# One table of the order for the whole program, and experts and Mamba as two lanes with buffers of their own

## What is computed

```python
x = x + 0.5 * ffn(LN(x)); x = x + mamba(LN(x)); x = x + 0.5 * ffn(LN(x))      # LN without weights

def ffn(x):                       # the same weights in both uses
    h = causal_conv3(layernorm(x)); q, k, v = split(h @ attn_w)               # 16 heads of 8
    x = x + softmax(causal(rope(q) @ rope(k).T / sqrt(8))) @ v @ proj_w
    h = layernorm(x); e = argmax(h @ router_w)                                # one of 4 experts for each token
    return x + (silu(h @ wv[e][:, :512]) * (h @ wv[e][:, 512:])) @ expert_proj[e]

def mamba(x):                     # convolution of 4 taps and silu give xs, B, C; 4 heads of 64, state of 64
    z, xs, B, C, dt = project(x @ W_in)
    for t in range(512): h = dA[t] * h + dt[t] * xs[t] * B[t]; y[t] = h @ C[t] + D * xs[t]
    x = x + rmsnorm(y * silu(z)) @ W_out
    return x + silu(rmsnorm(x) @ w1 + b1) @ w2 + b2
```

## Time and profile before

| | |
|---|---|
| median of 3 runs | 1969.23 us (1958.37 to 1971.66) |
| profiled execution, its own time | 1961.06 us |
| its span | 1959.3 us |
| TensorE matmuls busy | 1472.6 us, 75% |
| TensorE weight loads busy | 779.5 us, 40% |
| VectorE busy | 1202.9 us, 61% |
| ScalarE busy | 808.2 us, 41% |
| GpSimd busy | 386.4 us, 20% |
| mean granted clock of TensorE | 0.848 of full speed |
| attention core C0, first to last exponential | 81.7 to 129.3 us |
| C1 | 230.1 to 305.4 us |
| C2 | 403.8 to 489.0 us |
| C14 | 1710.6 to 1763.8 us |
| C15 | 1835.6 to 1889.5 us |
| Mamba of rows 3, 4, 5, 6: `mu` made at | 780.9, 985.3, 1192.7, 1397.9 us |

### The profile page before, as it was taken

How to read it: one execution, slowest core, us unless ns; L and a number is a source line. 1 busy time by engine, 2 the same in 40 slices (tenths; PEclk the granted TensorE clock), 3 DMA queues, 4 the chain that set the end, 5 groups by cost and what they waited for, 6 DMA issues and landing times. The chain is left out here.

```text
span 1959.3 us, 30365 instructions
## 1 busy us (share of the span) xinstructions
PE 1472.6 (75%) x11328; PEld 779.5 (40%) x11328; DVE 1202.9 (61%) x2807; ACT 808.2 (41%) x1266; POOL 386.4 (20%) x396
## 2 busy tenths in 40 slices
PE   1366686578787898788978897879788987773855
PEld 0133343334343454444534453435344544332423
DVE  5344654476649675876678667867685648543532
ACT  0132243334353445444545454355545451441432
POOL 1001131031113211231223022402141214011111
PEclk9578598868788899899979897899888987886877
DMA  5203000202020303031301130032103100302101
GB/s 166 27 2 62 1 2 17 46 1 33 22 42 2 48 29 62 2 43 27 62 8 27 22 74 16 7 43 49 35 7 43 31 22 6 42 22 39 24 9 33
DMA packets 75807, 61.43 MB, mean 31 GB/s; under 512 B 6800, under 2 KB 71824, under 8 KB 75664
## 3 DMA queue, kind: packets, MB, share of 16 engines
q1 hardware_dynamic: 71568, 51.10, 14.8%
q0 software_dynamic: 4096, 8.40, 1.4%
HBM read 19.23 MB, written 14.55 MB: 17 GB/s over the span
## 5 line engine op out<-in xcount | busy, mean ns | idle before, releaser
L907 ACT ACTIVATE prob_mem<-aring 128x1024 f32<-128x1024 f32 x320 | 325.5, 1023 | 208.9 <-PE aring L639 203.3
L1266 DVE TENSOR_REDUCE mx<-aring 128x2 f32<-128x1024 f32 (+2 forms) x384 | 316.9, 861 | 138.3 <-PE aring L622 136.1
L597 PE MATMUL aring<-ramps,spots 64*128 64x128 bf16 (+1 forms) x2560 | 182.3, 223 | 137.1 <-DVE mx L1266 56.9
L729 PE MATMUL wring<-wv,scratch 128*128 x448 | 238.2, 646 | 6.8 <-ACT scratch L944 3.6
L597 PEld LDWEIGHTS aring<-ramps,spots 64*128 64x128 bf16 x2560 | 87.9, 99 | 339.8 <-issue 201.5
L582 PE MATMUL obank<-prob_mem,vx 128*9 128x512 f32 (+3 forms) x2048 | 199.7, 491 | 25.3 <-ACT prob_mem L907 15.0
L859 ACT ACTIVATE scratch<-wring 128x512 f32<-128x512 f32 x224 | 97.9, 437 | 179.7 <-PE wring L734 127.4
L1080 POOL DMA_INDIRECT got<-od,slot x64 | 63.3, 988 | 491.8 <-DMA od<-scratch 468.3
L1377 DVE SCALAR_TENSOR_TENSOR scratch<-scratch,wring 128x512 f32<-128x512 f32 x112 | 76.9, 686 | 135.0 <-ACT scratch L949 133.9
L639 PE MATMUL aring<-stq,stk 50*128 50x512 bf16 (+3 forms) x1024 | 141.5, 335 | 0.0
L622 PE MATMUL aring<-stk,stq 48*128 48x128 bf16 (+3 forms) x1024 | 137.0, 330 | 0.0
(11 more groups left out here) (211 smaller groups left out, 2429.2 us busy)
## 6 DMA issues: line engine op xcount, KB each, us to landing
hb<-hd SPq DMA_DIRECT2D x16, 448.0 KB, 3.5
stq<-high SPq DMA_DIRECT2D x96, 64.0 KB
stk<-high SPq DMA_DIRECT2D x96, 64.0 KB
stq<-mid SPq DMA_DIRECT2D x64, 64.0 KB
stk<-mid SPq DMA_DIRECT2D x64, 64.0 KB
od<-scratch SPq DMA_DIRECT2D x16, 256.0 KB, 3.0
od<-scratch SPq DMA_DIRECT2D x16, 192.0 KB, 2.1
x<-in_x SPq DMA_DIRECT2D x8, 256.0 KB, 2.8
```

The costliest lines, as they stand in the source:

```text
L597: pe.matmul(dst, spots[rows, 2 * by_key + part, :], ramp, start=(part == 0), stop=False, skip_group_check=True)
L729: last = pe.matmul(ring[:], hTd[:, u * P:(u + 1) * P], wv[:, expert[u], o:o + DFF], start=True, stop=True)
L907: act.activation(prob_mem[:, k], ring[:], ACT.Exp, scale=float(HD) ** -0.5).then_inc(freed, 1)
L1266: last = dve.tensor_reduce(mx[:, j, h0 + q:h0 + q + 3:2], ring[:, :, c:c + w], AX_X, ALU.max)
```

## The change

The lanes are now seven: Mamba (number 3) and the experts (number 4) have one each, and G and L become 5 and 6. `plan` joins the lanes of all turns first, and `ORDER` has one digit for each of the 1952 steps, so no two turns need be alike. Which steps exist, and the order within each lane, are as before.

Because a Mamba step may now stand beside an expert step, `yv`, `yaT` and `ob` get tiles of their own, `hTd` takes the place of `hb` itself, `scratch` shrinks to 4 x 512 columns for `MV` and `ga`, and Mamba's `Xd`, `Xw`, `Gm`, `gb` and `gt` move into tiles of Mamba that are free at that time. With this go: `Xw` in two instructions, the two `Square`s of the Mamba tail both behind `Y1`, the load of `hb` behind the last `value` of the pass before, and a wait of `xsT` for the two `z` steps.

```diff
-            steps("M", i - 1, first=M_CUT) + steps("E", i - LAG - 1, 1) + steps("E", i) + steps("M", i, last=M_CUT),
+            steps("M", i - 1, first=M_CUT) + steps("M", i, last=M_CUT),
+            steps("E", i - LAG - 1, 1) + steps("E", i),
...
 ORDER = (
-    "11311121331233131321133311233133112302113113112331111331021033003310031131131501033331113110331031130311131311"
...
+    "00000000000000111111111111111101011111111111110111111111011101001111112111212121202221016101111111140110141404"
...
-    out = []
-    for i in range(-1, rows + LAG + 1):
-        lanes = [iter(lane) for lane in turn(i, rows)]
-        out += [(lane, *step) for lane in map(int, ORDER) if (step := next(lanes[lane])) is not None]
-        assert all(next(lane, None) is None for lane in lanes)
+    turns = [turn(i, rows) for i in range(-1, rows + LAG + 1)]
+    lanes = [iter([step for steps in turns for step in steps[lane] if step is not None]) for lane in range(len(turns[0]))]
+    out = [(lane, *next(lanes[lane])) for lane in map(int, ORDER)]
+    assert all(next(lane, None) is None for lane in lanes)
...
-        scratch = sb("scratch", [P, 8 * T])
-        hTd = scratch[:, 0:UNITS * P]
-        at = UNITS * P
-        yv = [scratch[:, at + T * k:at + T * (k + 1)] for k in range(2)]
-        yaT = [scratch[:, at + T * (2 + k):at + T * (3 + k)] for k in range(2)]
-        ob = scratch[:, 6 * T:6 * T + UNITS * P].rearrange("p (u c) -> p u c", u=UNITS)
+        hTd = hb[:].rearrange("p u c -> p (u c)")
+        yv = [sb(f"yv{k}", [P, T]) for k in range(2)]
+        yaT = [sb(f"yaT{k}", [P, T]) for k in range(2)]
+        ob = sb("ob", [P, UNITS, P])
...
+        scratch = sb("scratch", [P, 4 * T])
+        MV = scratch[:].rearrange("p (j h t) -> p j h t", j=4, h=MH)
...
-        Xd = scratch[:, 4 * T:6 * T].rearrange("p (j h d) -> p j h d", j=4, h=MH)
-        Xw = scratch[:, 6 * T:8 * T].rearrange("p (j h d) -> p j h d", j=4, h=MH)
+        Xd = [zt[k][:].rearrange("p (j h d) -> p j h d", j=2, h=MH) for k in range(2)]
+        Xw = [cpad[1 + k][:, 3:].rearrange("p (j h d) -> p j h d", j=2, h=MH) for k in range(2)]
...
-        Gm = sb("Gm", [P, 4, P])
+        Gm = uT[:].rearrange("p (j c) -> p j c", j=4)
...
-        gb, gt = ([scratch[:, T * (q + k):T * (q + k + 1)] for k in range(2)] for q in (4, 6))
+        gb, gt = ([conv[:, q + k] for k in range(2)] for q in (0, 2))
...
                 if n > 0:
-                    sp.wait_ge(s["w_filled"], w_fill["E", n - 1]["hb", 1] + 1)
+                    sp.wait_ge(s["w_filled"], w_fill["E", n - 1]["value", UNITS - 1] + 1)
...
-                    elif kind in ("Y0", "Y1"):
-                        c = int(kind == "Y1")
-                        act.wait_ge(s["m_gT"], 2 * i + c + 1)
-                        act.activation(gq[c][:], gT[c][:], ACT.Square).then_inc(s["m_gq"], 1)
+                    elif kind == "Y1":
+                        act.wait_ge(s["w_filled"], filled)
+                        for c in range(2):
+                            act.wait_ge(s["m_gT"], 2 * i + c + 1)
+                            act.activation(gq[c][:], gT[c][:], ACT.Square).then_inc(s["m_gq"], 1)
...
-                        pool.wait_ge(s["e_stored"], 32 * (ffn(0, i, NB) + 1))
...
+                        if c == 0:
+                            w_used(dve, step["z", 0], step["z", 1])
```

36 lines of the change are left out of this document (26 added, 10 removed).

## The result

The changed kernel takes 1730.84 us, median of four runs (1725.48 to 1734.06), against 1963.8 us (1955.4 to 1971.66) for the kernel before on the same chip. The ratio is 0.8812, 95% interval 0.876 to 0.8863. So it is faster by 233 us, where 139 were forecast and 1765 us was the lower end of the range. The direction was right, the size was not.

A forecast was written before the change was run, and what follows sets the result against it. TensorE, busy 1472.6 us, bounds the kernel; an order can win its 486.7 us idle. Fill −66, steady −55 and drain −18 sum to −139: 1961 to 1820 us, range 1785 to 1855 (54%), 1765 to 1895 for 8 in 10.

The forecast's parts named there:

- Buffers: The new buffer sharings and the later wait of the `hb` load, whole kernel: costed at nothing.
- Opening and end: Stretches to 129.3 us and from 1763.8 us on: 0, as C0 runs alone and the tail order stays.
- Two reloads of `hb` that nothing can cover: In the tail from C14 on: their 28.0 us of TensorE waits would stay.
- Fill: 129.3 to 574.1 us: −66 us, waits −58, clock −12, new `mlp` wait +4, with C1 and C2 spread over other lanes.
- mlp: New TensorE wait right behind `up` 3, about 2 us a row: +4 in the fill, +10 steady, +2 in the drain.
- Steady: 574.1 to 1598.5 us, five turns: −55 us, waits −71, `mlp` +10, VectorE beside GpSimd +6; `mx` drains stay.
- the +6 for VectorE beside GpSimd: Steady turns: GpSimd's Mamba products slow VectorE work beside them, some two such hits more a turn, +6 us.
- I take −12 for the 318.9 us of the stretch: Fill: a higher clock takes 12 us off TensorE's 318.9 us of busy time there.
- the sum treats each wait apart: Whole forecast: the −139 us adds up each wait's saving separately.
- Rival 1: More than forecast: denser order lifts the fill's clock to 0.9, −35 instead of −12, steady waits to 60: 1770 us, 15%.
- Rival 2: Steady gain lost to VectorE slowed beside GpSimd: 1865 us, 1875 with the gain gone, 1905 with half the fill; 20%.
- Rivals 3 and 4: 3: no change within 1%, idle time only moves, 6%; 4: slower, gates' banks held longer, 2000 us, 5%.

The follow-up runs named there:

- e1_old_order: Changed kernel with its new buffers and waits but the old list, five loads of `hb` 11 entries later: 1972.02 us, ratio 1.0001 to the kernel before.
- r2: Changed kernel with 54 of its 64 shifts moved right behind the last maximum of their group: 1883.97 us, ratio 0.9593 to the kernel before.
- r3: Changed kernel with 25 shifts moved up to about their old distance behind the last maximum: 1799.13 us, ratio 0.9138 to the kernel before.
- e2: Changed kernel with the new list up to the end of C4, then the old order: 1898.41 us, ratio 0.9629 to the kernel before.
- e3: Changed kernel with the old list up to the end of C4, then the new order: 1857.36 us, ratio 0.9425 to the kernel before.
- e4_one_lane: Changed kernel with Mamba and experts in the one sequence of the kernel before, other lanes near their new places: 2122.41 us, ratio 1.0808.
- c3_before_warm_long: Kernel before with idle transposes ahead of TensorE's long pauses only, none ahead of the shifts: 1982.5 us, ratio 1.0062.
- c1_before_warm: Kernel before with 836 idle transposes, four ahead of each of 64 shifts and more ahead of long pauses: 1954.71 us, ratio 0.993.
- c4_again: Changed kernel with four idle transposes ahead of each shift, run a second time: 1729.51 us, ratio 0.8768 to the kernel before.
- after_again: Changed kernel as it is, run again in the same session on another chip: 1730.43 us, ratio 0.8776 to the kernel before.

## Why the prediction was half right

**What bounds the kernel: right.** TensorE in order, waiting on short chains. Idle time gives 173 of the 233 us, the waits named in the earlier trace rows are the ones that went, and `e1_old_order` shows that nothing but the order did it.

**Buffers, opening, end.** Buffers at nothing: right (ratio 1.0001). Opening and end at 0: they brought 7 us, but 25 us of idle time went there (82.1 → 70.7 and 82.7 → 68.6) and was filled by work from elsewhere. "Two reloads of `hb` that nothing can cover" was wrong for one of the two.

**Fill.** Idle −57.6, where the waits and `mlp` summed to −54. C1's first exponentials came at 150.1 us (forecast: near 150) and C2's last at 355.5 (before 400). Clock 0.84 (over 0.82). The size agrees, the terms only in part: `mx` fell by 14.3 us (19.2 → 4.9) though the sum has no term for it, `mu` by 26.0 for the 20.8 forecast, the shift by 3.8 for 4.6, and against these `y` and `hn` grew by 12 us (1.9 → 7.5, 1.2 → 7.4). With the caution on the moved matmuls, this step was right in its mechanism and lucky in its number.

**Steady.** Idle −69 instead of −55: `mx` fell by 16 where it was left unchanged, `mlp` cost little (TensorE's wait for its product 6.7 us in all, 3.2 before: +3.5, where +16 was priced, 4, 10 and 2 in the three stretches), and the +6 for VectorE beside GpSimd had the wrong sign, as `CT` got out from under GpSimd's product in seven of eight rows. Against that `stq` kept 12.5 us instead of 3, and `mu` and `pick` came in new with 14.5 us. And TensorE's busy time fell by 35.5 us where the sum had none; that is what made 184 us a turn out of the 190 to 196 that were named.

**The two steps that failed.** First, the sentence "I take −12 for the 318.9 us of the stretch", and no such term anywhere else: TensorE's busy time was held constant in the steady turns, the drain and the end, as if idle time alone could go. It fell by 60.5 us, 48 more than forecast, and idle time by 46 more (172.9 against 127); the two make up the 94 us that were missing. In the table above busy time goes along with idle time, at equal matmuls: between before and after 60.5 / 172.9 = 0.35 us of busy time for each us of idle time, from r2 to after 53 / 94 = 0.56, from r3 to after 32 / 39 = 0.8. It isn't a fixed rate (e2, e3 and r2 have some 410 us idle each and 1444 to 1475 us busy); in that table it follows the cold us more closely, with (1485.8 − 1412.1) / (627 − 381) = 0.30 us for each between `e1_old_order` and the changed kernel, though not where idle transposes change the clock. I had the rows for it: the earlier trace rows show one group at 908 ns in the fill and 632 ns in the steady turns. I used them in the fill alone, since the steady turns already had a clock of 0.91; yet 2 × 0.09 × 1024 is 184 us at 1.2 GHz.

Second, "the sum treats each wait apart". Undone one at a time, the terms don't have the prices of their waits: `sm_a` 37 us of wait for 15.5 us of time, the shift 36 us of wait for 68 us. I read this from the list: Mamba's row is one of two independent lanes and has slack within the turn, while the shift is in the attention lane, where the copy, its DMA, the group's exponentials and the next core hang on it, with every lane's TensorE steps behind.

**The rivals.** Rival 1 (the clock, 1770 us, 15%) came nearest, and should have been the main forecast or have had its price in it: it assumed a fill at 0.9, and the fill is at 0.84; the busy time came down mostly in the steady turns and the drain instead (35.5 and 34.3 us, part of it for matmuls that moved; in the fill by 9.0, and in the opening and the end it rose with theirs). Its own −35 isn't what its words give: 632 against 908 ns is 30%, and of 159 us that is 48. Rival 2 (VectorE) is dead: its busy time went from 1202.9 to 1184.0 us, where over 40 more was the mark. The Trainium skill says in "SBUF — State Buffer", section "SBUF: two separate sides", that VectorE with two SBUF inputs and GpSimd hold a shared pair of ports in turn, each for a whole instruction. The eight `CT` products agree with that: 1.42 us each time that one stood within GpSimd's product, 0.69 us each time that it didn't. But the new order has fewer such meetings for them, not more. Rivals 3 and 4 needed waits that grow in place of the old ones. Those that grew are far too small: for the gates' banks (`yv`) TensorE waits 3.7 us in all instead of 2.3, and the largest that grew are `hn`'s 12 us and the gates' 9 for the copy of `hb`. A bad order with these buffers and banks is possible all the same, as `e4_one_lane` shows, but its waits are for `mu` and the shift, not rival 4's.

**What stays open.** How the 233 us split into clock and chain. Idle transposes are an imperfect test: they warm TensorE and occupy it. In the kernel before they bought 13 to 22 us, or cost 11 with the long pauses alone, in `r3_shift_as_before` they bought 31, in the changed kernel nothing. The 53 us that come only with both new stretches are explained by the seam in part, and not measured. That filling long pauses raised the clock of the fill and yet left the steady turns at 0.88, below the 0.91 before, and 29 us longer, I can't explain.

## What to carry to other kernels

In a list that TensorE works in order, price what a new order removes in two columns, the waits and the busy time: here each us of idle time removed took another 0.35 us of busy time with it, spread over Mamba's and the attention's groups and `proj`, with nothing in the experts'. A wait's sum is not its price: here it was under half of it in the lane with slack (15.5 us for 37) and nearly twice of it for the shift (68 us for 36). Test it by moving only that step back to its old distance. And a list is tuned as a whole: its two halves brought 69 and 110 us, the whole 233, and plausible local changes (a later shift, a packed tail) cost 35 and 40.

## What the runs showed of the hardware

- Matmuls of the same form differ with the order around them: `proj` 365 ns before and 296 after, while the experts' have 646 and 648. A mean granted clock of 0.91 still left some 22 us in 867 to be had (35.5 less the 13 for moved matmuls).
- Short pauses counted: those ahead of the shifts were 1.3 us on average (58 waits, 74.7 us). With only the long pauses filled the mean clock was 0.853 (0.848 before), with only the short ones 0.856, with both 0.883.
- The Trainium skill has in "TensorE: Matmul & The Clock Gate", section "HAM oscillation — how this bites in real kernels", that a wait which is long enough makes TensorE start again at the lower clock, and puts the cost at half of the time spent there. The traces agree on the sign. On the price they don't: 128 fewer cold us between `c3_before_warm_long` and `c1_before_warm` went with 28 us of time, and 65 fewer between `after_again` and `c4_again` (0.886 → 0.905) with 1 us. The cold us here also count time in which TensorE was idle or made idle transposes.
- Cheaper matmuls are not a shorter kernel: in `c4_again` the real matmuls' groups add up to 28 us less than in `after_again`, and the time fell by 1 us.
- The VectorE product `CT` (64x512) took 1.42 us all nine times that it stood within GpSimd's product on `upto`, and 0.69 us all seven times that it didn't (both kernels). That product, four instructions, took 4.99 us or more in such a meeting, and 4.03 to 4.49 us without one.
